# Attention and mixture-of-experts block on one core: new step lists for the first and middle batches, and the exponential biased by the negated maximum alone

## The reference

```python
x = x + tanh(g_xattn[0]) * xattn(layernorm(x), ctx_512, Wq, Wk, Wv, Wo, bo)
x = x + tanh(g_ffn[0]) * ffn(layernorm(x), gate_w, expert_w, expert_b)
...
scores = einsum('bhnd,bhmd->bhnm', qh, kh) * scale
attn = softmax(scores, axis=-1)
out = einsum('bhnm,bhmd->bhnd', attn, vh)
```

## Time and profile before

| | us |
|---|---|
| median of 3 runs | 945.15 (944.91 to 945.45) |
| the profiled execution | 948.67 |
| its span, first to last instruction | 946.9 |
| PE busy in the span | 902.7 (95%) |
| DVE busy | 852.6 (90%) |
| ACT busy | 743.8 (79%) |
| POOL busy | 646.3 (68%) |
| TensorE clock granted, mean | 0.987 of full |

### The profile page before, as it was taken

The page is one execution under the profiler, slowest core; times in us unless marked ns, Lnnn a source line. Parts: engine busy times, 40 slices in busy tenths (PEclk is TensorE's granted clock), DMA queues, the critical chain, the costliest instruction groups (busy, mean ns, idle before and its releaser), DMA issues.

```text
span 946.9 us, 28867 instructions
## 1 busy us (share of the span) xinstructions
PE 902.7 (95%) x11376; PEld 605.1 (64%) x11376; DVE 852.6 (90%) x1853; ACT 743.8 (79%) x1093; POOL 646.3 (68%) x449
## 2 busy tenths in 40 slices
PE   6788799999999999999999999999999999999997
PEld 4245455777657776677657776577655776667873
DVE  6899799998999989999899989999899998999768
ACT  3898899778995879958896879958899588988510
POOL 4677768677695867768586776958687686877400
PEclk9899899999999999999999999999999999999999
DMA  6699899999999999989999999989999799999900
GB/s 222 143 179 167 146 161 190 165 150 165 171 193 149 158 148 197 183 141 157 180 180 160 153 162 189 186 146 157 150 187 187 137 154 171 169 169 164 143 24 23
DMA packets 549142, 150.97 MB, mean 159 GB/s; under 512 B 537592, under 2 KB 547216, under 8 KB 548752
## 3 DMA queue, kind: packets, MB, share of 16 engines
q1 hardware_dynamic: 549008, 149.13, 94.7%
HBM read 11.70 MB, written 4.19 MB: 17 GB/s over the span
## 4 chain that ended last, share of the span: by engine, by line
PE 47%; DVE 25%; ACT 12%; issue 8%; DMA 3%; POOL 3%; SPq 1%; ACTq 0%; DVEq 0%; POOLq 0%
PE MB L1338 24%; PE ST L1480 9%; PE PV L1502 9%; DVE nmax L1021 8%; ACT pf L832 5%; ACT p_s L842 4%; PE MB L1350 3%; DMA pt_s<-p_s 3%; POOL p_s L654 2%; DVE acc L956 2%; DVE QL L1001 2%; DVE x L924 1%; DVE o_n L1044 1%; DVE v_s L1012 1%; ACT v_s L758 1%
## 5 line engine op out<-in xcount | busy, mean ns | idle before, releaser
L654 POOL TENSOR_TENSOR p_s<-pf,p_s 128x1024 f16<-128x1024 f32 x254 | 542.1, 2136 | 217.3 <-ACT p_s L842 169.1
L832 ACT ACTIVATE pf<-ST,shifts 128x512 f32<-128x512 f32 x512 | 324.4, 691 | 92.2 <-DVE shifts L1027 89.9
L1021 DVE TENSOR_REDUCE nmax<-ST 128x2 f32<-128x1024 f32 x256 | 310.4, 1217 | 17.6 <-PE ST L1480 15.8
L842 ACT ACTIVATE p_s<-pf 128x1024 f16<-128x1024 f32 x254 | 270.7, 1069 | 3.2
L1502 PEld LDWEIGHTS PV<-v_s,pt_s 128*128 128x128 f16 x6096 | 204.3, 98 | 43.6 <-issue 27.5
L1502 PE MATMUL PV<-v_s,pt_s 128*128 128x65 f16 x6096 | 215.7, 193 | 4.7 <-DVE o_n L1044 2.7
L1338 PE MATMUL MB<-ex_s,x2t_s 128*128 128x256 f16 (+1 forms) x1380 | 166.8, 276 | 1.1 <-DVE x L924 1.0
L1338 PEld LDWEIGHTS MB<-ex_s,x2t_s 128*128 128x128 f16 x1380 | 131.7, 98 | 23.6 <-DVE x L924 2.3
L1480 PE MATMUL ST<-KH,QH 64*128 64x512 f16 x512 | 100.8, 390 | 16.3 <-ACT pf L832 14.0
L975 DVE SCALAR_TENSOR_TENSOR acc<-MB,m,acc 128x256 f32<-128x256 f32 x224 | 95.6, 476 | 4.4 <-PE MB L1338 3.6
L1480 PE MATMUL ST<-KH,QL 64*128 64x512 f16 x512 | 99.0, 383 | 0.0
(11 more groups left out here) (174 smaller groups left out, 986.5 us busy)
## 6 DMA issues: line engine op xcount, KB each, us to landing
pt_s<-p_s SPq DMA_TRANSPOSE x508, 3.4
xin<-x SPq DMA_DIRECT2D x7, 512.0 KB, 4.9
out<-acc SPq DMA_DIRECT2D x7, 512.0 KB, 3.9
kvin<-kv_t SPq DMA_DIRECT2D x8, 256.0 KB, 4.4
stage_e<-expert_t SPq DMA_DIRECT2D x1, 2048.0 KB, 11.1
stage_o<-wo SPq DMA_DIRECT2D x1, 1024.0 KB, 5.8
stage_q<-wq SPq DMA_DIRECT2D x1, 768.0 KB, 7.3
xin<-x SPq DMA_DIRECT2D x2, 256.0 KB, 2.9
```

Of the source, the lines that this page charges most:

```text
L654: pool.tensor_tensor(p_s[:, slot, 1, :, :], pf[:, it.ring(p, u, PF_SLOTS), :, :], p_s[:, slot, 0, :, :], ALU.subtract).then_inc(p_lo, 1)
L832: last = act.activation(pf[:, (n - 1) % PF_SLOTS, i, :], ST[u % 2][:, i, :], ACT.Exp, bias=shifts[:, u % 2, i:i + 1])
L842: act.activation(p_s[:, it.ring(p, u, P_SLOTS), 0, :, :], pf[:, it.ring(p, u, PF_SLOTS), :, :], ACT.Copy).then_inc(p_hi, 1)
L1021: dve.tensor_reduce(nmax[:, t % 2, :, 0], ST[t % 2][:, :, :], AX.X, ALU.max, negate=True)\
```

## The change

Two things are changed. DVE's `shift` step goes in all eight batches: `nmax` loses its constant word, ACT waits on `max_done` in place of `shift_ready` and reads `nmax` as its bias. One memset on POOL goes with it. The step lists of the FIRST and LOOP batches are written anew on all four engines, with the same number of steps of each kind apart from `shift`. The lists of the LAST batch are those of before, without `shift`.

```diff
-P_SHIFT = 7 * math.log(2.0)
...
-        nmax = sb("nmax", [P, 2, 2, 2])
-        shifts = sb("shifts", [P, 2, 2])
+        nmax = sb("nmax", [P, 2, 2])
...
-            pool.memset(nmax[:, :, :, 1], P_SHIFT).then_inc(const_pool, 1)
...
-                act.wait_ge(shift_ready, n)
+                act.wait_ge(max_done, n)
                 act.wait_ge(p_lo, n)
                 for i in range(2):
                     last = act.activation(pf[:, (n - 1) % PF_SLOTS, i, :], ST[u % 2][:, i, :], ACT.Exp,
-                                          bias=shifts[:, u % 2, i:i + 1])
+                                          bias=nmax[:, u % 2, i:i + 1])
...
-                dve.tensor_reduce(nmax[:, t % 2, :, 0], ST[t % 2][:, :, :], AX.X, ALU.max, negate=True)\
+                dve.tensor_reduce(nmax[:, t % 2, :], ST[t % 2][:, :, :], AX.X, ALU.max, negate=True)\
                    .then_inc(max_done, 1)
-
-            def shift_of(b, p, t):
-
-                dve.wait_ge(max_done, unit_count(b, p, t))
-                dve.tensor_reduce(shifts[:, t % 2, :], nmax[:, t % 2, :, :], AX.X, ALU.add).then_inc(shift_ready, 1)
```

Of the tables one line of each sign shows the manner (FIRST on DVE):

```diff
-        "maximum shift rq", "maximum shift pt", "maximum take shift", "maximum normalise take take shift",
+        "maximum rq", "maximum pt", "maximum take", "maximum take take", "maximum lm take",
```

More of the change, by code:

```diff
@@ L129 @@
     FIRST: (
-        "maximum shift rq", "maximum shift pt", "maximum take shift", "maximum normalise take take shift",
-        "maximum lm shift lm normalise", "maximum take shift", "maximum lm shift take take",
-        "maximum bound normalise shift lm", "maximum normalise shift", "maximum take take shift",
-        "maximum take shift lm take", "maximum normalise shift", "maximum take lm shift",
-        "maximum take shift normalise ls", "maximum take shift", "maximum normalise sums1 shift",
@@ L140 @@
-        "maximum take shift ll take take take",
+        "maximum rq", "maximum pt", "maximum take", "maximum take take", "maximum lm take",
+        "maximum take lm", "maximum normalise take lm", "maximum take lm",
+        "maximum normalise take bound", "maximum normalise normalise take",
+        "maximum take take normalise lm", "maximum normalise lm", "maximum take",
+        "maximum ls normalise sums1", "maximum",
+        "maximum take moments1 normalise ll take take take normalise", "maximum",
@@ L141 @@
+        "maximum take ll ll ll", "maximum take take normalise", "maximum ll take",
+        "maximum take ll", "maximum take", "maximum take take normalise", "maximum ll take",
+        "maximum normalise take", "maximum take normalise ll take", "maximum normalise gp",
+        "maximum take take ll normalise take", "maximum take ll ll", "maximum take",
+        "maximum take take take", "maximum ll normalise take take take",
     ),
     LOOP: (
-        "maximum shift", "maximum shift normalise", "maximum take shift take normalise",
@@ L155 @@
-        "maximum take take shift normalise take take",
+        "maximum", "maximum normalise take", "maximum take normalise take", "maximum take bound",
+        "maximum take normalise", "maximum take normalise take take", "maximum take",
+        "maximum take", "maximum take take sums2 normalise moments2", "maximum take",
+        "maximum normalise take take take", "maximum take take take",
+        "maximum normalise take take take", "maximum take take normalise take",
+        "maximum take sums1 take", "maximum take normalise route1 take",
@@ L168 @@
-        "maximum shift take take take take take take normalise take take take",
+        "maximum", "maximum normalise take", "maximum take normalise",
+        "maximum take take normalise", "maximum take take", "maximum take",
+        "maximum take take normalise", "maximum take take", "maximum sums2 moments2",
+        "maximum normalise take", "maximum take take take normalise",
+        "maximum take take normalise take take", "maximum take take take", "maximum take route1 take",
+        "maximum", "maximum normalise take route2 take normalise", "maximum route3 take take",
@@ L1188, in before @@
             def before(it):
-                count.update(take=0, shift=0, maximum=-MAXIMUM_BACK, normalise=-NORMALISE_BACK)
+                count.update(take=0, maximum=-MAXIMUM_BACK, normalise=-NORMALISE_BACK)
             def row(it, n):
@@ L1217, in row @@
                             maximum(b, *divmod(at, TT))
-                    elif part == "shift":
-                        if kind == FIRST and at == 0:
-                            dve.wait_ge(const_pool, CONST_POOL)
-                        shift_of(b, *divmod(at, TT))
                     elif part == "normalise":
```

106 lines of the change are left out of this document (44 added, 62 removed), and 3 rows, old and new, of the table PE_ORDER.

## The result

The changed kernel takes 951.8 us (median of 6 runs, 950.26 to 953.62) beside 945.03 us (943.66 to 947.99) for the kernel before on the same chip: a ratio of 1.0071, 95% interval 1.0053 to 1.0088. It is slower by 6.7 us (0.71%, clear of the interval), where 8.3 us less were forecast. The profiled execution took 953.18 us, its span is 951.4 us.

A forecast was written before the change was run, and what follows sets the result against it. PE was taken to bound the middle and last batches, a loop of nearly full DVE and ACT the first. -5.4 (first), -2.4 (middle) and -0.5 (last) sum to -8.3 us: 936.9 us from 945.15, range 931 to 944.5.

The forecast's parts named there:

- The hole: First batch: ACT's `context` stood 3.62 us for `c_mul`; the new order removes the wait, 3.4 us less (0 to 3.6).
- 32 shifts: First batch: 32 fewer `shift` steps on DVE at 0.07 us each, 2.0 us less (0 to 6.4).
- The rest of the new lists: First batch: same number of steps, so worth only the waits: 0, from -3.5 to +3.5 us.
- Rival D: The twelve `ll` steps meet POOL's subtractions: 20 us more (957 us), or three fully hit, 5 us (942); chance 0.04.
- The middle batches: Six batches: two thirds of PE's idle goes, added score runs cost 0.4 us: -0.4 each, -2.4 us (-4.8 to +3.0).
- Rival C: High parts ahead of unit 15's exponential make ACT wait for PE; slower, 951.3 us at 2 us per middle batch; chance 0.06, shared.
- The last batch: Order kept, shifts gone, 1.2 us of PE's idle can be touched: -0.5 us (-1.5 to +0.5).

The follow-up runs named there:

- e8: e1 with ScalarE's `context` moved from row 20 to 24 and GpSimd's from row 25 to 26 of the first batch: 938.46 us, ratio 0.9927.
- e1: The kernel before without `shift`, all old step lists kept: 943.01 us, ratio 0.9970 to the kernel before.
- e3: The kernel before without `shift`, with the new lists of the middle batches only: 946.93 us, ratio 1.0015 to the kernel before.
- e10: e3 with four `values` steps of the middle batches placed later, and two `normalise` steps that wait for them: 941.64 us, ratio 0.9956.
- e2: The kernel before without `shift`, with the new lists of the first batch only: 946.76 us, ratio 1.0016 to the kernel before.

## Why the prediction was wrong

- **The views were read rightly.** The first batch was bound by VectorE and ScalarE in a loop, the middle ones by TensorE: the missing `shift` gave these nothing (656.7 to 663.3 us for the six in the nine traces with the old middle lists, 659.8 before).
- **The hole, -3.4 us: right.** e8 gives -4.1 (1.4 to 6.7). The price was the smallest idle time in the rows.
- **32 shifts, -2.0 us: right as far as it can be told.** 2.8 us for all shifts (interval 0.9 to 4.7), of which 0.8 lie in the last batch of the traces. The first batch alone fell by 2.9 us in e1's trace and by 4.6 to 5.4 in those of e3 and e10, so single traces don't fix its share. The kernel's time fits the estimate by start-to-start times (0.07 us each) better than 0.15 us each, which gave 4.8. That price was no rule of the page: the Trainium skill ("VectorE: DVE Perf Modes", "The DRAIN you can't avoid") adds that a next operation which is not held starts earlier, and the 0.07 us agree with that.
- **"The rest of the new lists", 0 us with bounds of 3.5 either way: the step that failed.** The new lists without the hole end 8.4 us above the old lists without the hole, and 5.6 of them go with the second SBUF input of the `ll` steps. I priced a whole reshuffle by saying that the number of steps is the same. What isn't the same is what runs beside them: the twelve `ll` steps grew from 14.3 to 18.3 us, and three of them now fell where a maximum was due, with TensorE's next job behind it. Rival D named the meetings, with the right mechanism and the right place, and gave them 4%: its two sizes, 5 and 20 us, were worked out, and then set aside because the mean before was 1.33 us. But the mean before was the mean at the old places. Neither D nor the sum had a term for what follows a stop of TensorE: in e2 3.4 us of stop and then 6.8 us at the lower clock, although showed a granted clock of 0.91 in this stage. The forecast also set D's 5 us against a gain of 8.3 and so kept "faster" even if D came.
- **The middle batches, -2.4 us: the second step that failed, wrong in sign.** The lists cost +4.3 (some 2 to 6.5). I counted runs of `scores` and the idle time that could be won, and never asked of each `values` step how many units lay between it and its exponential. The bad bound, +3.0, was reached by adding 0.1 us per batch to the idle; a wait of 2 us at a place with no slack wasn't in it.
- **Rival C** had the place where ScalarE waits, and the waits came (2.09 us at unit 14 to 15). By its own sum the slack was 2.6 and 0.8 us, and that held: in e3 TensorE is never stopped by an exponential behind them.
- **The last batch, -0.5 us:** 93.4 us before and 92.6 after up to the last maximum, -0.8. Right.
- **The chances.** 0.86 for faster came from a sum in which both big stages had an unpriced reshuffle with symmetric bounds. The first came out far beyond the bad bound (8.4 against 3.5), the middle one beyond it too (4.3 against 3.0), though not clear of noise.

## What to carry to other kernels

An order written anew is not worth "the number of steps is the same": for each moved step ask what it waits for and how many units that lead is now, and what runs on the other engines beside it. A gain found in a trace (here one step that waited for a value made two units later) should be cut out and made alone; it gave 4 us for two moved steps, and the rewrite of the same stage round it ended 8 us above that. A late step is worth its length only if no other engine stops behind it: here one stop of TensorE was followed by a stretch at half the clock. And a wait on an engine with time to spare is no loss until something is shown to stand behind it: moving the steps at which ScalarE waited cost 16 us.

## What was not expected of the hardware

- A two-input VectorE step with both in SBUF lasted 0.74 us alone and up to 2.64 us when it began inside GpSimd's subtraction, ending about 0.55 us behind it every time but six in 115, and 3.23 us behind two subtractions in a row. The subtraction that began beside such a step went from 2.14 to 2.33 us. Reducing one input to the same size lasted 0.67 to 0.68 us beside GpSimd or not.
- A short stop of TensorE can cost more than itself. In the fourth middle batch of the change TensorE waited 1.81 us for a transfer, and the granted clock of the next 3.2 us was at the lower of its two levels, 1.2 GHz; e3 waited 1.48 us at the same place, and its clock stayed. The length alone doesn't decide it: a wait of 1.97 us in the change's sixth middle batch left the clock full. Stretches before, at and after it in the change:

```profile
470.00:483.00 13.00, 11.60 (x178) 6.92 (x174) 11.78 (x19) 13.00 (x21) 9.86 (x5) 1.00 1.13 198
484.20:487.40 3.20, 3.20 (x16) 1.11 (x13) 1.23 (x1) 1.00 (x3) 1.76 (x1) 0.50 1.03 194
488.00:500.00 12.00, 12.00 (x161) 7.48 (x159) 11.00 (x24) 9.91 (x15) 10.20 (x11) 1.00 0.99 166
```

There the six matmuls of a unit's scores took 1.39 us (484.23 to 485.62) in place of 0.75 us. This is one more reason why the `values` steps cost the middle batches more than the length of their waits: those 3.2 us ran at half speed, some 1.6 us of work lost by estimate.
